# One mixing group ahead of the edge counting, and the input's splitting spread over five tiles

## Time and profile before

| | |
|---|---|
| median of the runs | 1123.69 us (1123.31 to 1125.04, three runs) |
| the profiled execution | 1121.66 us, span 1119.9 us, mean granted TensorE clock 0.955 |
| TensorE matmul busy | 993.3 us, 89% of the span |
| VectorE, ScalarE, GpSimd busy | 686.4, 381.7, 82.0 us |
| counting phase | to about 280 us; the first matmul of the first dense stage (L649) starts at 291 us |

### The profile page before, as it was taken

How to read it: one execution, slowest core, us unless ns; L and a number is a source line. 1 busy time by engine, 2 the same in 40 slices (tenths; PEclk the granted TensorE clock), 3 DMA queues, 4 the chain that set the end, 5 groups by cost and what they waited for, 6 DMA issues and landing times.

```text
span 1119.9 us, 15330 instructions
## 1 busy us (share of the span) xinstructions
PE 993.3 (89%) x4904; PEld 478.9 (43%) x4904; DVE 686.4 (61%) x1351; ACT 381.7 (34%) x550; POOL 82.0 (7%) x66
## 2 busy tenths in 40 slices
PE   3998999975799799778996579899999999999997
PEld 1444444432445554233442234444444444445443
DVE  6657556565245673876888789989752225642358
ACT  1322222256477552134211452211432221324442
POOL 1000000023003100011000320000220000100100
PEclk9999999988899899889998889999999999999999
DMA  6554655501022010644455425545100013310114
GB/s 217 171 163 127 205 166 156 169 19 38 1 74 79 29 57 23 202 134 150 113 160 178 131 63 172 153 130 160 38 1 20 1 36 116 95 46 11 38 31 156
DMA packets 62614, 112.80 MB, mean 101 GB/s; under 512 B 7617, under 2 KB 8086, under 8 KB 62554
## 3 DMA queue, kind: packets, MB, share of 16 engines
q1 hardware_dynamic: 52634, 94.15, 27.6%
q10 hardware_dynamic: 9920, 17.83, 4.9%
HBM read 99.43 MB, written 12.52 MB: 100 GB/s over the span
## 4 chain that ended last, share of the span: by engine, by line
PE 65%; DVE 20%; ACT 6%; DMA 4%; issue 3%; POOL 1%; DVEq 0%; ACTq 0%; SPq 0%; POOLq 0%
PE Dp L649 20%; PE Dp L674 20%; PE Dp L552 9%; PE T L593 8%; DVE acc L1123 8%; PE Dp L696 4%; PE T L625 2%; DVE stt L1207 1%; PE T L575 1%; DMA stage<-in_basis 1%; DVE Zraw L1228 1%; DVE w L1247 1%; ACT A L736 1%; DVE S L1195 1%; DVE Zraw L1187 1%
## 5 line engine op out<-in xcount | busy, mean ns | idle before, releaser
L649 PE MATMUL Dp<-W,hT 128*128 128x512 f16 x1560 | 356.9, 386 | 13.0 <-POOL W L494 7.0
L649 PEld LDWEIGHTS Dp<-W,hT 128*128 128x128 f16 x1560 | 151.9, 99 | 189.2 <-issue 17.1
L674 PE MATMUL Dp<-Zraw,AT 128*128 128x512 f16 x600 | 144.4, 404 | 38.2 <-DVE w L1247 38.2
L674 PE MATMUL Dp<-Zraw,A 128*128 128x512 f16 x800 | 173.3, 379 | 0.0
L1123 DVE SCALAR_TENSOR_TENSOR acc<-stage,att,acc 128x512 f32<-128x512 f32 x232 | 156.5, 743 | 18.2 <-DMA stage<-in_basis 18.2
L552 PE MATMUL Dp<-Zraw 128*128 x594 | 118.7, 358 | 25.0 <-DVE Zraw L1053 20.3
L674 PEld LDWEIGHTS Dp<-Zraw,A 128*128 128x128 f16 x800 | 78.2, 98 | 93.9 <-DVE w L1247 0.2
L674 PEld LDWEIGHTS Dp<-Zraw,AT 128*128 128x128 f16 x600 | 60.9, 103 | 120.0 <-DVE w L1247 42.2
L1047 DVE SCALAR_TENSOR_TENSOR Zraw<-w,hT 128x256 f16 x99 | 50.5, 510 | 98.0 <-PE Dp L552 84.3
L593 PE MATMUL T<-Zraw,W 128*128 128x512 f32 x240 | 108.1, 598 | 0.3
L1053 DVE TENSOR_SCALAR Zraw<-hT,w 128x1280 f16 x198 | 104.5, 570 | 0.0
(11 more groups left out here) (150 smaller groups left out, 747.8 us busy)
## 6 DMA issues: line engine op xcount, KB each, us to landing
Zraw<-in_basis SPq DMA_DIRECT2D x120, 256.0 KB, 3.2
stage<-in_basis SPq DMA_DIRECT2D x120, 256.0 KB, 2.8
xres<-w ACTq DMA_DIRECT2D x30, 256.0 KB, 2.0
xr<-xres ACTq DMA_DIRECT2D x30, 256.0 KB, 2.6
stage<-in_Wn SPq DMA_DIRECT2D x16, 256.0 KB, 2.9
stage<-in_Ws SPq DMA_DIRECT2D x16, 256.0 KB, 2.9
stage<-mixd SPq DMA_DIRECT2D x16, 256.0 KB, 3.1
stage<-in_root SPq DMA_DIRECT2D x16, 256.0 KB, 3.0
```

The costliest lines, as they stand in the source:

```text
L649: last = nc.tensor.matmul(Dp[:, j, m, :], hT[:, j, hp, k * P:(k + 1) * P], W[:, m, wp, k, :], start=(n == 0), stop=(n == 3 * KT - 1))
L674: last = nc.tensor.matmul(Dp[:, j, 2, :], a[:, k, ds(t * P, P)], Z[:, r, h, k, :], start=(n == 0), stop=(n == count - 1))
```

## The change

It does three things.

1. All 15 matmuls of mixing group 0 are run before the first window. Groups 1 to 7 are mixed in tiles 0 to 6 (7 and 8 matmuls at the windows, as before). Tiles 7, 8 and 9 mix nothing. SyncE loads group 0 ahead of x.
2. Each tile 4 to 8 splits two tiles of x: one right behind the copy of its first window, one behind the copies of its second. The block of five before tile 8 and the block of five before tile 9 go.
3. VectorE looks for the largest |x| between windows 3 and 4, and sets the scale between windows 6 and 7.

```diff
-MIX_AT = {w: (PAIRS // 2 if w % 2 == 0 else PAIRS - PAIRS // 2) for w in range(2 * GROUPS)}
+MIX_AT = {w: (PAIRS // 2 if w % 2 == 0 else PAIRS - PAIRS // 2) for w in range(2 * GROUPS - 2)}
...
+        XS_FROM = 4
...
                 sp.dma_start(attp[b2 * 64:(b2 + 1) * 64, :], att1[b2:b2 + 1, :].broadcast_to([64, BASES])).then_inc(e_att, 16)
+            def load_mix(g):
+                for b in range(PAIRS):
+                    n = g * PAIRS + b
+                    wait(sp, s_mx, n - MIX_SLOTS + 1)
+                    sp.dma_start(mix_in[n % MIX_SLOTS], basis1[g, b, :, :]).then_inc(mx_full[n % MIX_SLOTS], 16)
+
+            load_mix(0)
             sp.dma_start(acc_x, x[0:XA * P, :].rearrange("(t p) d -> p t d", p=P)).then_inc(e_x, 16)
...
-                        for mix_group in range(4):
+                        for mix_group in range(1, 4):
...
+            mix(PAIRS)
             for t in range(NT):
                 half = MIX_AT.get(2 * t, 0)
...
             def tile_out(t):
+                first = (t - XS_FROM) * 2
                 window_out(t * 2, 0, t)
+                if 0 <= first < NT:
+                    split_x(first)
                 if t:
                     turned_out(t - 1, 0)
                     turned_out(t - 1, 1)
                 window_out(t * 2 + 1, 1, t)
                 if t:
                     turned_out(t - 1, 2)
-                if t < GROUPS:
-                    mixed_out(t)
+                if 0 <= first < NT:
+                    split_x(first + 1)
+                if t < GROUPS - 1:
+                    mixed_out(t + 1)
...
-            for t in range(NT - 2):
+            mixed_out(0)
+            for t in range(NT):
+                if t == XS_FROM:
+                    act.wait_ge(s_s0, 1)
+                if t == NT - 1:
+                    high_weights(0, 0, 1)
                 tile_out(t)
-            act.wait_ge(s_s0, 1)
-            for t in range(0, 5):
-                split_x(t)
-            tile_out(NT - 2)
-            for t in range(5, NT):
-                split_x(t)
-            high_weights(0, 0, 1)
-            tile_out(NT - 1)
...
-            windows(0, 6)
+            windows(0, 4)
...
-            windows(6, 12)
+            windows(4, 7)
...
-            windows(12, NWIN)
+            windows(7, NWIN)
```

More of the change, by code:

```diff
@@ L386, in _ @@
                 sp.dma_start(tile[:, :], vec).then_inc(s_bn, 16)
[L387 to L391, removed]
             seen = set()
```

## The result

The changed kernel takes **1130.32 us** (median of five runs, 1129.85 to 1134.17); the kernel before takes 1123.69 (five runs, 1121.94 to 1125.04). The ratio is 1.0072, with a 95% interval of 1.0059 to 1.0085: slower by 6.6 us, where 7.0 were forecast. The profiled execution was the shortest of the five, 1129.85 us, with a span of 1128.1 against 1119.9.

What follows compares the result with a forecast made beforehand. TensorE's own work was taken to bound the mixing tiles, waits tiles 8 and 9. The terms 8.8 + 3.0 + 4.0 - 8.8 gave +7.0 us on 1123.69, so 1130.7 us, range 1120.5 to 1136.

Steps and rivals of the forecast that it cites:

- group in front, end of window 0: At the start: mixing group 0 first makes window 0 end at 35.2 instead of 26.42 us, +8.8 us.
- loads of group 1: Before window 1: base loads queued behind x arrive late and less work is queued ahead of the window, +3.0 us.
- splits, tiles 4 to 6: Each tile's first split on ScalarE pushes TensorE's turn by 1.32 us, +4.0 us over three tiles.
- tiles 7 to 9: 21.1, 23.5, 18.1: Rebuilt lengths in us of the three tiles without mixing: together 62.7 against 71.5, -8.8 us.
- search moved: Search for the largest |x|, two windows earlier: same place in a tile, same 4.7 us price, so 0.
- The 2.0 us for the slow start: Front group's first matmuls: charged as running slowly after the start, 2.0 us within the +8.8.
- 2.0 us of wait: After window 0: TensorE wants group 1's first load at 35.3 us, but it lands at 37.3.
- The 1.0 us for window 1 losing its lead: Window 1: less work queued ahead behind the load wait, 1.0 of a possible 2.4 us.
- "issue" gaps: Windows with nothing queued ahead: TensorE's sequencer computing addresses and branches before single pairs, 2.4 us more a window.
- The rival in which bare windows run at full speed: Windows 15 to 18 take 5.57 us each, 9.6 us less: -2.6 us in all, 1121.1 us; chance 0.13.
- The one in which the clock falls in tiles 4 to 6: Windows 9, 11 and 13 slow down after TensorE's pauses, 2.6 us each: +14.8 in all, 1138.5 us; chance 0.09.

Runs made afterwards that it cites:

- run 7: The changed kernel with 35 extra f16 matmuls, results unused, ahead of everything on TensorE, ending about when the table is ready: 1130.58 us.
- run 1: The changed kernel with x loaded behind the first eight loads of mixing group 0 instead of behind all fifteen: 1124.73 us, ratio 1.0032.
- run 2: The changed kernel with the first split of each of tiles 4 to 8 moved behind the second turned copy: 1124.86 us, ratio 1.0023.
- run 4: The kernel before with splitting spread over tiles 4 to 8, first splits late, search moved with it, no front group: 1115.74 us, ratio 0.9935.
- run 8: The changed kernel with four f32 matmuls, results unused, added right ahead of each of windows 15 to 19: 1143.31 us.
- run 9: The changed kernel with three f32 matmuls, results unused, added between the first and second turn of tiles 7 to 9: 1134.99 us.
- run 11: run 10 with VectorE's search cut in two, W0's maximum behind window 3 and x's behind window 5: 1118.51 us, ratio 0.9955.
- run 12: run 4 with VectorE's search cut in two, W0's maximum behind window 3 and x's behind window 5: 1110.55 us, ratio 0.9886.
- run 10: run 4 with mixing spread evenly, 12 or 13 matmuls a tile in tiles 0 to 8 and seven in tile 9: 1120.42 us, ratio 0.9979.
- run 6: The changed kernel with 26 extra f16 matmuls, results unused, ahead of everything on TensorE: 1130.04 us, ratio 1.0066.

## Why the prediction was right

Its steps, against the two traces. The sum at the end of window 19 was +7.0 and came out at 288.44 - 279.68 = +8.8; behind it the profiled execution gave back 0.6, so the spans differ by 8.2, and the medians by 6.6. The mechanism was forecast and is short by 1.8; that the medians land within 0.4 us of the forecast is partly luck.

| step | forecast | traced | settled by |
|---|---|---|---|
| group in front, end of window 0 | +8.8 | +8.9 | run 7 |
| loads of group 1 | +3.0 | +4.7 | run 1 |
| splits, tiles 4 to 6 | +4.0 | +3.9 | run 2 |
| tiles 7 to 9: 21.1, 23.5, 18.1 | -8.8 | -8.9 | runs 4, 8, 9 |
| search moved | 0 | 0 | runs 11, 12 |

The first step was right by two errors that cancel: the table was ready at 13.44, 0.9 us before what the trace of before had, and window 0 took 6.70 us instead of 5.57, with a gap before its last pair (6.70 = 4.79 + 0.67 + 1.24). The 2.0 us for the slow start were right (2.2 by run 7), though in run 1's execution it was longer: the group took 16.03 us there, against 15.24.

The loads are the term that was mis-sized. "2.0 us of wait" were 3.33, because group 1's first load was issued at 29.63 instead of 28.6: x was issued at 22.32, earlier than forecast, but from there to the first base SyncE took 7.31 us instead of the 5.26 of the kernel before (W0's four issues alone 2.95 instead of 1.89). The time to landing, 9.0, was near the 8.7 forecast. The 1.0 us for window 1 losing its lead was a wrong mechanism: it lost none (5.58 us), and instead the seven matmuls took 1.5 us longer at the half clock that came with the wait. The prediction thought of the clock only at the start and in tiles 4 to 6. In other executions the term was larger: window 1 started at 48.12 and 50.07 us in runs 8 and 9, which have the same code up to there; the waits were 4.17 and 5.67 us, and the granted clock in the mixing behind them 0.69.

The third step was right in its sum: with 0.07 us of slack in the earlier trace rows, a split of 1.32 us on ScalarE lengthens the tile. The three terms were 1.65, 1.15 and 1.13 us rather than 1.32 each; in tile 4 ScalarE also began the copy of the window 0.4 us late. The search kept its price: window 4 starts after 2.09 us of idleness and takes 8.21.

The rebuilding of tiles 7 to 9 rested on one reading, that "issue" gaps are a cost of a bare window and not of tile 9. Runs 8 and 9 show it from both sides. The prediction's case for the reading was weaker than it looked: that VectorE is busy for 11.01 of 22.85 us doesn't exclude waits for it, and "windows 1 to 16 all do" (run at 5.57) overlooks window 6 with its 8.15. The rival in which bare windows run at full speed fell with windows 15 to 18 at 7.9, 8.0, 7.8 and 8.2 us. The one in which the clock falls in tiles 4 to 6 fell too: windows 9, 11 and 13 kept 5.57 us behind pauses of 1.66 us and less, with the granted clock at 1.00 from 41.73 us to 225. It also laid window 6's slowness to the clock. In the changed kernel window 4, in the same place, takes 8.21 us with the granted clock at 1.00, and in run 1 8.21 at 0.79, so there the clock costs nothing.

The Trainium skill's rule, "TensorE: Matmul & The Clock Gate", Part 1, that the half rate is the default and activity releases it, was weighed against the profile's granted clock of 1.00 at the start. The runs side with the page: the group took 15.24 us from idleness and 13.04 behind matmuls.

## What to carry to other kernels

Work that fills waits is worth more than its own time, and moving it costs what it covered: before moving a batch, list the waits that it hides where it is (here a copy on another engine, 3.6 us, and a sequencer's lead, 2.4 us a window) and those that it will hide where it goes. An engine that isn't the bound can still have a position in its order with no slack; look for the step that ends last before the bound engine's wait, and put new work behind it, not ahead. A new wait can cost more than its length: behind the one of 3.33 us, the half clock took another 1.5. When a load is moved behind others that wait for compute, everything queued behind it on that engine moves too.

## What the runs showed of the hardware that was not expected

- A loop on TensorE with addresses from registers can cost its sequencer more than its array: six matmuls that take 1.08 us when queued took 1.7 to 1.9 us a pair when not (from the second pair on, run 9, granted clock 1.00). Over five pairs even a half-rate start disappeared behind that (window 15: 7.90 us at a clock of 0.85, 7.86 at 1.00); over the three of window 19 it did not (5.75 and 4.35 us).
- The length of a pause alone didn't decide whether the half clock came. Behind 2.18 us of waiting in tile 5, five mixing matmuls ran at 1.00 in run 10 and at 0.72 in run 11, 4.56 and 6.19 us. Behind the pause of 2.1 us at the search the window ran at 0.79 in the kernel before and in run 1, at 1.00 in the changed kernel. Pauses of 1.66 us and less in tiles 4 to 6 of the changed kernel were not followed by it.
- The profile's granted clock reads 1.00 from the span's start, although the first matmuls run at half rate: in the changed kernel the instructions of the front group start 0.8 to 1.0 us apart until 17.89 us, and 0.43 from there on. Only when work preceded (run 6) did the record show the half clock.
